# Tensor product with the features on partitions: x turned on TensorE, spherical rows repeated by transfers, one chunk of four by GpSimd

## The reference

```
h   = relu(layernorm(x))                       # 3125 x 64
wk  = mlp2(edge_attr_64, k_w1, ...)            # E x 128, wv likewise
k   = sum_s sh[:, s] * (h[src] @ Cqk[:, s, :]) * wk      # s = 0..8
v   = sum_s sh[:, s] * (h[src] @ Cv[:, s, :])  * wv
attn = einsum over 16 features of q[segment] and k            # E x 8 heads
alpha = segment softmax of attn ; upd = segment sum of v * alpha
out = h @ W_self + upd @ W_out, normalised over the nodes
```

## Time and profile before

| | |
|---|---|
| median of 3 runs | 3731.14 us (3730.2 to 3732.13) |
| profiled execution | 3729.88 us, span 3728.2 us, mean granted TensorE clock 0.942 |
| busy of the span | PE 3330.0 us (89%), weight loads 3178.9 (85%), VectorE 2877.5 (77%), ScalarE 1285.0 (34%), GpSimd 2055.4 (55%) |
| transfers | 622.16 MB, mean 167 GB/s |

### The profile page before, as it was taken

One profiled execution on the slowest core, in us unless ns is written; L12 is line 12 of the kernel. 1 busy time (PEld: TensorE's weight loads), 2 busy tenths in 40 slices (PEclk: granted clock), 3 DMA queues, 4 the chain that ended last, 5 costly groups with the idle time before them and its releaser, 6 DMA issues. The chain is left out here.

```text
span 3728.2 us, 86642 instructions
## 1 busy us (share of the span) xinstructions
PE 3330.0 (89%) x25947; PEld 3178.9 (85%) x25947; DVE 2877.5 (77%) x5292; ACT 1285.0 (34%) x3333; POOL 2055.4 (55%) x1999
## 2 busy tenths in 40 slices
PE   2099999999999337999999999999999999999963
PEld 1088888888888237999999999999999999999953
DVE  4366666666666227999999999999999999999943
ACT  1033333333333113444444444444444444444420
POOL 2577777777777435555555555555555555555540
PEclk9599999999999658999999999999999999999975
DMA  8399999999999313444444444444444444444420
GB/s 339 86 268 280 279 279 279 279 280 279 279 280 279 105 46 105 127 126 132 131 124 129 131 129 124 130 132 126 125 132 132 124 128 131 130 124 129 132 78 29
DMA packets 843789, 622.16 MB, mean 167 GB/s; under 512 B 490431, under 2 KB 732803, under 8 KB 843452
## 3 DMA queue, kind: packets, MB, share of 16 engines
q1 hardware_dynamic: 667110, 500.09, 44.2%
q0 software_dynamic: 56640, 87.65, 9.7%
q10 hardware_dynamic: 119982, 33.79, 4.1%
HBM read 335.87 MB, written 286.31 MB: 167 GB/s over the span
## 5 line engine op out<-in xcount | busy, mean ns | idle before, releaser
L1305 POOL DMA_INDIRECT xg<-h_tab,src_i x808 | 861.5, 1066 | 220.8 <-issue 127.2
L789 POOL DMA_INDIRECT kv<-kv_tab,src_i x808 | 762.1, 943 | 285.7 <-issue 188.2
L1315 POOL TENSOR_TENSOR kq<-kvs,q_of 128x512 f32<-128x512 f32 x202 | 260.6, 1290 | 837.7 <-DVE kvs L1491 837.7
L1401 ACT ACTIVATE z_hi<-bank 128x512 fp32r<-128x512 f32 x808 | 439.4, 595 | 802.9 <-PE bank L1333 802.9
L1357 PE MATMUL bank<-C_hi,z_hi 128*128 128x256 f32 x4040 | 682.2, 299 | 0.0
L1357 PE MATMUL bank<-C_lo,z_hi 128*128 128x256 f32 x4040 | 612.2, 281 | 0.0
L1481 DVE TENSOR_TENSOR z_lo<-bank,z_hi 128x512 fp32r<-128x512 f32 x808 | 520.5, 686 | 113.5 <-ACT z_hi L1401 113.4
L1357 PEld LDWEIGHTS bank<-C_hi,z_hi 128*128 128x128 f32 x4040 | 537.8, 191 | 0.3
L1357 PEld LDWEIGHTS bank<-C_lo,z_hi 128*128 128x128 f32 x4040 | 535.3, 188 | 0.0
L1357 PE MATMUL bank<-C_hi,z_lo 128*128 128x256 f32 x3232 | 516.2, 281 | 0.0
L913 DVE TENSOR_TENSOR wsb<-bank,b 128x512 f32<-128x512 f32 x404 | 279.3, 691 | 298.7 <-PE bank L977 298.3
(11 more groups left out here) (248 smaller groups left out, 4754.4 us busy)
## 6 DMA issues: line engine op xcount, KB each, us to landing
w_tab<-wsb SPq DMA_DIRECT2D x202, 512.0 KB, 3.4
win<-w_tab SPq DMA_DIRECT2D x202, 512.0 KB, 3.6
sum_edge<-rowt SPq DMA_DIRECT2D x202, 288.0 KB, 2.5
q_edge<-zq SPq DMA_DIRECT2D x202, 256.0 KB
qs<-q_edge SPq DMA_DIRECT2D x202, 256.0 KB, 2.8
sum_edge<-rows ACTq DMA_DIRECT2D x202, 136.0 KB
qs<-q_edge SPq DMA_DIRECT2D x202, 128.0 KB
drow<-dst_tab SPq DMA_DIRECT2D x202, 128.0 KB, 3.2
```

The source lines that it names most:

```text
L789: pool.indirect_dma_start(kv[b][:, q, :], None, kv0_tab, bass.IndirectOffsetOnAxis(ap=src_i[:, i * Q + q:i * Q + q + 1], axis=0))\
L1305: pool.indirect_dma_start(xg[b][:, q, :], None, h1_tab, bass.IndirectOffsetOnAxis(ap=src_i[:, i * Q + q:i * Q + q + 1], axis=0))\
L1315: pool.tensor_tensor(kq[:, :].rearrange("p (q o) -> p q o", q=Q), kvs[b][:, :, 0:O1], q_of[b % 2][:, :].rearrange("p (q o) -> p q o", q=Q) ...
L1401: nc.scalar.activation(z_hi[b % 2][:, k, :], bank[ZB[k]][:, :], ACT.Copy).then_inc(hi_out, 1)
```

## The change

- **Layout.** z is made with (s, d) on partitions from the start. TensorE turns only xg (`turn_x`, 2 blocks a step, into bank 0 or 1), ScalarE copies the result to both halves of the partitions (`take_x`, four 64x256 copies) as `xT`. `sh` is now 128 x 4 x 512: partitions 0 to 63 hold the values s = 0, 2, 4, 6 of each of the 512 edges, partitions 64 to 127 s = 1, 3, 5, 7, the same in each partition of a half. `sh_last` holds s = 8, 256 edges in either half.
- **Transfers.** `load_sh` issues four broadcast DMAs a step (two of 64 x 1 KB, two of 64 x 8 KB) from two new tables in device memory.
- **Tables.** The node stage before the loop builds them: SyncE loads edge_attr_9 as 2 x 101 rows of 18 KB, ScalarE copies each half into the order s, edge (three copies), SyncE stores them.
- **Products.** VectorE's `outer` does three chunks of z in one 128x1536 instruction, GpSimd's `z_part` does the fourth (128x512), VectorE's `outer_last` the fifth (two of 64x256).
- **Casts and rests.** hi and lo are now two instructions of 128x1024 each, and read z in SBUF, not a PSUM bank; hi_last and lo_last are two of 64x256 each.
- **Banks and order.** spread_q writes a bank of its own (2). The four engines' lists have a new order; gathers run 5 steps ahead, not 4.

The diff, cut to its core:

```diff
+                    def load_sh_rows(a):
+                        last_full = (NST - 1) * ST
+                        sp.dma_start(sh_rows[0][:, :, :], a[0:SG * ST, :].rearrange("(p e) s -> p e s", p=SG))\
+                          .then_inc(sh_rows_in, 16)
+                        sp.dma_start(sh_rows[1][0:NST - 1 - SG, :, :],
+                                     a[SG * ST:last_full, :].rearrange("(p e) s -> p e s", e=ST)).then_inc(sh_rows_in, 16)
+                        sp.dma_start(sh_rows[1][NST - 1 - SG:NST - SG, 0:TAIL, :], a[last_full:E, :].unsqueeze(0))\
+                          .then_inc(sh_rows_in, 16)
+
                     load_last_rows(sp, lrows, sum0_edge, last_got)
+                    sp.wait_ge(sh_padded, 1)
+                    sp.sem_inc(sh_rows_turn, 1)
+                    with sp.If(flag > 0):
+                        load_sh_rows(ea9_s)
+                    with sp.Else():
+                        load_sh_rows(ea9)
...
+                    for g in range(2):
+                        sp.wait_ge(sh_parts_set, g + 1)
+                        sp.dma_start(sh_tab[g * SG:(g + 1) * SG], sh_parts[:, 0:S - 1, :]).then_inc(sh_put, 16)
+                        sp.dma_start(sh_last_tab[g * SG:(g + 1) * SG, :], sh_parts[:, S - 1, :]).then_inc(sh_put, 16)
...
+                    act.wait_ge(sh_rows_in, 48)
+                    for g in range(2):
+                        if g:
+                            act.wait_ge(sh_put, 32)
+                        for r in range(2):
+                            nc.scalar.activation(sh_parts[:, 4 * r:4 * r + 4, :],
+                                                 sh_rows[g][:, :, r:S - 1:2].rearrange("p e c -> p c e"), ACT.Copy)
+                        nc.scalar.activation(sh_parts[:, S - 1, :], sh_rows[g][:, :, S - 1], ACT.Copy)\
+                                 .then_inc(sh_parts_set, 1)
...
-            sh = [sb(f"sh{b}", [P, Q, S], F32, ph) for b in range(RING)]
+            sh = [sb(f"sh{b}", [P, 4, ST], F32, ph) for b in range(2)]
+            sh_last = [sb(f"sh_last{b}", [P, ST // 2], F32, ph) for b in range(2)]
+            xT = [sb(f"xT{b}", [P, ST], F32, ph) for b in range(2)]
...
             rows = [sb(f"rowt{b}", [P, Q, F2], F32, ph) for b in range(RING)]
-            z = [sb(f"z{b}", [P, Q, (S - 1) * D], F32, ph) for b in range(2)]
-            z_last = [sb(f"z_last{b}", [P, Q * D], F32, ph) for b in range(2)]
+            z = [sb(f"z{b}", [P, 4, ST], F32, ph) for b in range(2)]
+            z_last = [sb(f"z_last{b}", [P, ST // 2], F32, ph) for b in range(2)]
...
-
                     def load_sh(it, i, b):
-                        need(sp, z_ready, (i - RING + 1) * 2)
-                        load_either(sp, sh_turn, flag, i, sh[b][:, :, :], ea9, ea9_s, sh_in[b], sh_tail)
+                        need(sp, z_last_ready, i - 1)
+                        for f, e in zip(rows_of, edges_of):
+                            sp.dma_start(sh_last[b % 2][f, :], sh_last_tab[bass.ds(i, 1), e].broadcast_to([D, ST // 2]))\
+                              .then_inc(sh_in[b % 2], 16)
+
+                        need(sp, z_part_ready, i - 1)
+                        for r, f in enumerate(rows_of):
+                            sp.dma_start(sh[b % 2][f, :, :].rearrange("p c e -> p (c e)"),
+                                         sh_tab[bass.ds(i, 1), 4 * r:4 * r + 4, :].rearrange("a c e -> a (c e)")
+                                         .broadcast_to([D, 4 * ST])).then_inc(sh_in[b % 2], 16)
...
-                        need(pool, z_ready, (i - RING + 1) * 2)
+                        need(pool, x_mm, i - RING + 1)
...
-                    unrolled([(times_q, -1), (gather_x, 4)], RING)
+                    def z_part(it, i, b):
+                        pool.wait_ge(x_out, i + 1)
+                        pool.wait_ge(sh_in[b % 2], 64 * (2 * it + b // 2 + 1))
+
+                        need(pool, lo_out, i * 3 - 4)
+                        pool.tensor_tensor(z[b % 2][:, ZD, :], xT[b % 2][:, :], sh[b % 2][:, ZD, :], ALU.mult)\
+                            .then_inc(z_part_ready, 1)
+
+                    unrolled([(times_q, -1), (z_part, 2), (gather_x, 5)], RING)
...
+                    def turn_x(it, i, b):
+                        pe.wait_ge(x_got[b], 16 * Q * (it + 1))
+
+                        need(pe, x_out, i - 1)
+                        for h in range(Q // 2):
+                            ins = nc.tensor.transpose(bank[b % 2][:, h * P:(h + 1) * P],
+                                                      xg[b][:, 2 * h:2 * h + 2, :].rearrange("p r d -> p (r d)"), ident[:, :])
+                        ins.then_inc(x_mm, 1)
...
-                        need(pe, below_ready, i - 1)
-                        need(pe, max_copied, i - 1)
+                        pe.wait_ge(qs_in[b % 2], 16 * (2 * it + b // 2 + 1))
+
+                        need(pe, q_taken, i)
                         for q in range(Q):
-                            ins = nc.tensor.matmul(bank[SHARED][:, q * O1:(q + 1) * O1], same[b][:, q, :], qs[b % 2][:, q, :],
+                            ins = nc.tensor.matmul(bank[SPREAD][:, q * O1:(q + 1) * O1], same[b][:, q, :], qs[b % 2][:, q, :],
                                                    start=True, stop=True)
...
-                    pipelined(pe, [(t_z(0), 1), (t_z(1), 1), (turn_max, -2), (sums, -3), (m_acc(0), 0), (t_z(2), 1),
-                                   (t_z(3), 1), (m_acc(1), 0), (t_z(4), 1), (spread_q, 0), (m_acc(2), 0),
-                                   (turn_logits, -1), (m_acc(3), 0)], RING)
+                    pipelined(pe, [(turn_x, 3), (turn_max, -2), (sums, -3), (m_acc(0), 0), (m_acc(1), 0), (turn_logits, -1),
+                                   (spread_q, 0), (m_acc(2), 0), (m_acc(3), 0)], RING)
...
+                    def take_x(it, i, b):
+                        act.wait_ge(x_mm, i + 1)
+
+                        need(act, z_last_ready, i - 1)
+                        need(act, z_part_ready, i - 1)
+                        for f in rows_of:
+                            for r, g in enumerate(rows_of):
+                                ins = nc.scalar.activation(xT[b % 2][f, :].rearrange("p (h r e) -> p h r e", r=2, e=P)[:, :, r, :],
+                                                           bank[b % 2][g, 0:2 * P].rearrange("p (h e) -> p h e", e=P), ACT.Copy)
+                        ins.then_inc(x_out, 1)
+
                     def hi(k):
                         def stage(it, i, b):
...
+                            act.wait_ge(z_ready, i + 1)
+                            if k == 1:
+                                act.wait_ge(z_part_ready, i + 1)
                             need(act, a_mm, i * 2 - 2)
...
+                            nc.scalar.activation(z_hi[b % 2][:, 2 * k:2 * k + 2, :], z[b % 2][:, 2 * k:2 * k + 2, :],
+                                                 ACT.Copy).then_inc(hi_out, 1)
                         return stage
+
+                    def hi_last(it, i, b):
+                        act.wait_ge(z_last_ready, i + 1)
+                        need(act, a_mm, i * 2 - 2)
+                        for f, e in zip(rows_of, edges_of):
+                            ins = nc.scalar.activation(z_hi[b % 2][f, 4, e], z_last[b % 2][f, :], ACT.Copy)
+                        ins.then_inc(hi_out, 1)
...
-                    pipelined(act, [(hi(0), 1), (hi(1), 1), (copy_max, -2), (weights, -2), (take_sums, -3), (hi(2), 1),
-                                    (hi(3), 1), (hi(4), 1), (take_q, 0)], RING)
+                    pipelined(act, [(hi(0), 1), (take_x, 3), (copy_max, -2), (weights, -2), (take_sums, -3), (hi(1), 1),
+                                    (hi_last, 1), (take_q, 0)], RING)
...
+                    def outer(it, i, b):
+                        dve.wait_ge(x_out, i + 1)
+                        dve.wait_ge(sh_in[b % 2], 64 * (2 * it + b // 2 + 1))
+
+                        need(dve, lo_out, i * 3 - 4)
+                        dve.tensor_tensor(z[b % 2][:, 0:ZD, :], bcast(xT[b % 2][:, :], 1, ZD), sh[b % 2][:, 0:ZD, :],
+                                          ALU.mult).then_inc(z_ready, 1)
+
+                    def outer_last(it, i, b):
+                        need(dve, lo_out, i * 3 - 3)
+                        for f, e in zip(rows_of, edges_of):
+                            ins = dve.tensor_tensor(z_last[b % 2][f, :], xT[b % 2][f, e], sh_last[b % 2][f, :], ALU.mult)
+                        ins.then_inc(z_last_ready, 1)
+
+                    def lo(k):
                         def stage(it, i, b):
...
+                            dve.wait_ge(hi_out, i * 3 + k + 1)
                             need(dve, a_mm, i * 2 - 2)
...
+                            c = slice(2 * k, 2 * k + 2)
+                            dve.tensor_tensor(z_lo[b % 2][:, c, :], z[b % 2][:, c, :], z_hi[b % 2][:, c, :].bitcast(F32),
                                               ALU.subtract).then_inc(lo_out, 1)
```

(51 more changed lines are left out.)

57 lines of the change are left out of this document (10 added, 47 removed).

## The result

The changed kernel takes 4023.56 us (median of 4 runs, 4022.58 to 4025.96) against 3731.64 us for the kernel before on the same chip: a ratio of 1.0783, 95% interval 1.0764 to 1.0801. That is 292 us slower. The prediction had slower, +145 us, within a range that holds the time; half of the loss was not foreseen. The profiled execution has a span of 4021.0 us against 3728.2. Every ratio in this document compares only those runs of a kernel that lie within 1.5% of its fastest one.

What follows compares the result with a forecast made beforehand. The prediction took VectorE to bound the loop: 9.39 us plus 2.0 of stall, 11.4 a step against 10.67, gives +141 us; with 4 before and at the loop's start, 3,876 us. Range 3,690 to 4,100.

Steps and rivals of the forecast that it cites:

- TensorE leaves the bound: In the loop, 16 transposes a step go, so TensorE needs 8.95 us a step and no longer sets it.
- VectorE's own 9.39 us: In the loop, VectorE's instructions sum to 9.39 us a step if it never waits.
- The stall of 2.0 by the two engines' SBUF reads: In each loop step, VectorE instructions with two SBUF inputs and GpSimd's SBUF-reading products exclude each other, costing 2.0 us.
- outer first: Order within a step: outer starts before kq, the reduction waits for kq, va for z_part; about 2.0 us.
- one-sided rival: In the loop, VectorE holds up GpSimd but is never held up: step 10.74 us, 3,750 us in all; chance 0.12.
- side-by-side rival: In the loop, both engines' products run together: step 9.39 us, 3,476 us, up to 3,640 if transfers limit; chance 0.15.
- Transfers in the loop at nothing: The loop's added broadcast transfers fit in the step and cost nothing, up to 1 us a step if late.
- the prediction's three prices: Transfer time for the loop's added rows: 2.8 us a step at best rate, 4.1 at loop rate, 5.4 at half ports.
- Loop's start, 2 us: Where the loop begins: turn_x and take_x ahead of the first outer, z_part(0) behind twelve gathers, fewer transposes; 2 us more.
- the part before the loop: Before the loop, building the tables (ScalarE's copies, SyncE's loads and stores) is mostly hidden: 0 to 10 us, taken as 2.
- The price of ScalarE's copies: Before the loop, ScalarE turns sh_rows into sh_parts in about 4.5 us for each half.

Runs made afterwards that it cites:

- the fastest version: Changed kernel with table transfers cut 96 and 5, no z_part, x gathered once, doubled by ScalarE at its step's end, read from PSUM: median 3698.06 us.

## Why the prediction was right in its sign and wrong in its size

- **TensorE leaves the bound** (8.95 us of 11.4): right. Weight loads are busy 403.18 of 500, 9.2 a step, at a granted clock of 0.97.
- **VectorE's own 9.39 us**: measured 11.40 - 1.68 = 9.72. The missing 0.33: the z_last and z_hi pairs of 64x256 last 0.84 to 0.85, about 0.87 and 0.89 start to start, where 0.66 and 0.77 were taken. The 0.33 apiece was the distance from a 128x256 to a longer instruction behind it; here each of the pair takes its whole 0.42, and 64 partitions are no cheaper than 128 (0.42 for 128x256 in the earlier trace rows). Outer, 1.74 with 1.66 start to start forecast, was right.
- **The stall of 2.0 by the two engines' SBUF reads**: right in place and order ("outer first", then z_part ahead of va); 1.68 measured, since kq had 1.15 left behind outer instead of 1.30, and va, started 0.67 behind z_part, had 0.47 to wait instead of 0.70. That VectorE's own work was 0.33 too low and the stall 0.32 too high is luck: it makes the 11.4 exact. The one-sided rival falls with va, the side-by-side rival with kq, and the versions with x in PSUM and with the memsets show the cause.
- **Transfers in the loop at nothing**: right for this kernel; no wait for sh, 7.2 us to land. The share was foreseen at 0.67 and is 0.87: 0.87 x 11.40 - 4.8 = 5.1 us a step for the added rows, nearest to the highest of the prediction's three prices (2.8, 4.1 and 5.4). It decides only once the step falls under 11, as in the x in PSUM version.
- **Loop's start, 2 us**: measured 8.7. The first outer starts 14.9 us after the first gather, where the first product started 8.1 after it: 6.8 of the 8.7.
- **The failed step** is in "the part before the loop": "SyncE loads 3.7 MB and stores it again" was given "0 to 10, I take 2". It measured 137 us in the trace and 133 alone. The idle 46 us of ScalarE were there, but neither half fitted: the first copy begins at 1332.71, and the second half's end at 1432.3, not near 1294, and the copies to wvT behind them carry the delay on to the loop. The bytes were priced as though all engines carried them: at the 29 GB/s of those stretches 1.8 MB alone take 62 us, ScalarE waits for the loads of both halves at once, and the second half waits for the first's store. The price of ScalarE's copies was short too: 7.55 + 1.09 = 8.6 us a half, 4.5 estimated. With 137 in place of 2 the forecast's sum is 3729.9 + 141 + 2 + 137 = 4,010; the start's 8.7 gives 4,017, and the loop's 148.6 in place of 141 the 4,022.7 of the profiled execution, to 2 us.

## What to carry to other kernels

Price a transfer by its outermost dimension before its bytes: 101 partitions cost 123 us here, and a leading 2 some 3,100. When work moves to GpSimd, list for each VectorE instruction beside it whether both read SBUF, and with how many operands; an operand left in PSUM takes the conflict away. Idle time on an engine that runs in order is no slack for a step that it waits for in the middle of its sequence; on TensorE such a wait cost twice here, since the granted clock behind it was 0.50.

## What the runs showed of the hardware that was not expected

- A GpSimd product that starts 0.05 us behind a VectorE instruction with two SBUF inputs lasts that instruction's length longer, less 0.2 (2.84 us behind 1.74, 3.38 behind 2.27, 1.30 behind a 2.27 with one input in PSUM); a GpSimd memset stretches nothing (va 682 ns).
- The VectorE instruction takes as long from PSUM as from SBUF: 2284 (2274 in the fastest version) and 2272 ns for 128x2048.
- GpSimd's gathers lasted 0.94 us undisturbed, 1.33 on average in the changed loop and 1.65 in the fastest version, and cost nothing there as long as what reads them stood last in its engine's order.
- The three versions whose profile shows a DMA share of 0.99 to 1.05 spread over 2 to 7% from run to run (3684 to 3810, 3718 to 3797, 3656 to 3920), where every version at up to 0.91 stayed within 0.7%. Why was not tested.
- After 3.66 us of idling in the loop, TensorE's granted clock was 0.50 for some 3 us (the version with the reduction moved).
